# Attention with P turned by DVE in 32x32 blocks, and the context summed in sixteen 32x32 tiles

## The reference

```python
def _lora_linear(x, W, A, B):
    return x @ W + SCALING * (x @ A @ B)
q = _lora_linear(hidden_states, Wq, Aq, Bq).reshape(bsz, q_len, NH, HD)
...
k = _lora_linear(traces, Wk, Ak, Bk).reshape(bsz, t_len, NKV, HD)
v = _lora_linear(traces, Wv, Av, Bv).reshape(bsz, t_len, NKV, HD)
...
scores = jnp.einsum('bhqd,bhtd->bhqt', q, k) / jnp.sqrt(jnp.asarray(HD, q.dtype))
attn = jax.nn.softmax(scores, axis=-1)
context = jnp.einsum('bhqt,bhtd->bhqd', attn, v)
context = jnp.transpose(context, (0, 2, 1, 3)).reshape(bsz, q_len, H)
out = _lora_linear(context, Wo, Ao, Bo)
return hidden_states + out
```

## Time and profile before

| | us |
|---|---|
| median of 3 runs (755.91 to 757.85) | 755.97 |
| span of the profiled execution | 753.1 |
| PE busy | 737.6 |
| DVE busy | 469.0 |
| ACT busy | 382.0 |
| POOL busy | 349.1 |
| second pass of the body loop (127.98 to 193.53) | 65.55 |

### The profile page before, as it was taken

The page is one execution under the profiler, slowest core; times in us unless marked ns, Lnnn a source line. Parts: engine busy times, 40 slices in busy tenths (PEclk is TensorE's granted clock), DMA queues, the critical chain, the costliest instruction groups (busy, mean ns, idle before and its releaser), DMA issues.

```text
span 753.1 us, 17856 instructions
## 1 busy us (share of the span) xinstructions
PE 737.6 (98%) x5776; PEld 645.2 (86%) x5776; DVE 469.0 (62%) x988; ACT 382.0 (51%) x1287; POOL 349.1 (46%) x322
## 2 busy tenths in 40 slices
PE   7899999999999999999999999999999999999998
PEld 6678899889989989999998998999867788888886
DVE  5957687687768668767876866787696412212211
ACT  4437665666666666666666666665685210111100
POOL 4757645745654574565557457555766100000000
PEclk9999999999999999999999999999999999999999
DMA  7775544554453555345454544645464834343331
GB/s 257 271 219 164 169 140 140 159 172 122 139 174 126 157 152 163 119 139 175 138 156 149 155 131 128 172 139 178 139 181 154 276 130 156 117 167 111 111 111 56
DMA packets 94665, 117.01 MB, mean 155 GB/s; under 512 B 8624, under 2 KB 76208, under 8 KB 94640
## 3 DMA queue, kind: packets, MB, share of 16 engines
q1 hardware_dynamic: 94640, 116.69, 49.3%
HBM read 78.91 MB, written 37.75 MB: 155 GB/s over the span
## 4 chain that ended last, share of the span: by engine, by line
PE 88%; DVE 5%; DMA 2%; issue 2%; POOL 1%; ACT 0%; SPq 0%; POOLq 0%; DVEq 0%
PE banks L868 32%; PE banks L917 23%; PE banks L897 15%; PE banks L906 8%; PE banks L882 7%; DVE neg_max L718 2%; PE banks L853 2%; DVE x_lo L725 2%; DMA probs_t<-wq 1%; PE banks L855 1%; DMA probs<-b4q 1%; DMA probs_t<-b4kv 1%; POOL k_stack L510 1%; DVE lora L679 0%; DVE probs_t L263 0%
## 5 line engine op out<-in xcount | busy, mean ns | idle before, releaser
L525 POOL TENSOR_TENSOR probs<-probs,rsums 128x512 f32<-128x512 f32 x256 | 266.4, 1041 | 205.4 <-DVE rsums L750 204.6
L582 ACT ACTIVATE probs<-banks,neg_max 128x256 f32<-128x256 f32 x512 | 238.7, 475 | 175.7 <-DVE neg_max L718 170.8
L718 DVE TENSOR_REDUCE neg_max<-banks 128x2 f32<-128x512 f32 x256 | 174.3, 682 | 20.0 <-PE banks L882 20.0
L897 PE MATMUL banks<-ident,probs 128*128 128x128 f32 x1024 | 157.1, 276 | 2.2 <-POOL probs L525 2.0
L263 DVE COPY probs_t<-banks 128x512 f32<-128x512 f32 x192 | 132.4, 690 | 43.0 <-PE banks L897 35.6
L868 PE MATMUL banks<-x_hi,w_hi 128*128 128x256 f32 x512 | 145.7, 285 | 0.8 <-POOL w_lo L500 0.4
L868 PE MATMUL banks<-x_hi,w_lo 128*128 128x256 f32 x512 | 144.6, 282 | 0.0
L868 PE MATMUL banks<-x_lo,w_hi 128*128 128x256 f32 x512 | 144.5, 282 | 0.0
L897 PEld LDWEIGHTS banks<-ident,probs 128*128 128x128 f32 x1024 | 115.5, 140 | 30.8 <-issue 27.1
L882 PE MATMUL banks<-k_stack,q_stack 96*128 96x256 f32 x512 | 122.8, 322 | 0.0
L582 ACT ACTIVATION_READ_ACCUMULATOR probs<-banks,neg_max 128x1 f32 x512 | 104.0, 203 | 0.0
(11 more groups left out here) (76 smaller groups left out, 1112.9 us busy)
## 6 DMA issues: line engine op xcount, KB each, us to landing
q_stack<-q_parts SPq DMA_DIRECT2D x192, 128.0 KB, 2.5
q_parts<-q_stage SPq DMA_DIRECT2D x64, 256.0 KB, 2.2
raw<-ct SPq DMA_DIRECT2D x32, 256.0 KB, 3.9
raw<-xt SPq DMA_DIRECT2D x32, 256.0 KB, 4.4
context<-ctx_stage SPq DMA_DIRECT2D x64, 128.0 KB, 1.8
probs<-xn SPq DMA_DIRECT2D x16, 512.0 KB, 4.1
out<-raw SPq DMA_DIRECT2D x15, 512.0 KB, 2.9
probs_t<-context SPq DMA_DIRECT2D x7, 1024.0 KB, 5.9
```

The lines of the kernel that those rows point to most:

```text
L525: nc.gpsimd.tensor_tensor(probs[:, c], probs[:, c], rsums[:, c, :].unsqueeze(2).broadcast_to([P, 2, S]), ALU.mult).then_inc(norm_done, 1)
L582: last = nc.scalar.activation(probs[:, c, h, :], score_bank[c][:, S * h:S * (h + 1)], ACT.Exp, bias=neg_max[:, c, h:h + 1], scale=-1.0, ac ...
L718: nc.vector.tensor_reduce(out=neg_max[:, c, :], in_=score_bank[c].rearrange("p (h t) -> p h t", h=2), axis=AXIS, op=ALU.min).then_inc(max_ ...
L897: last = nc.tensor.transpose(bank[:, P * (2 * t + h):P * (2 * t + h + 1)], probs[:, c, h, P * t:P * (t + 1)], ident[:])
```

## The change

P is no longer turned by PE. DVE turns each 32x32 block of a slot's tile in place of its row and column (`transpose`, from `probs` to `turned_p`), so that partition 32r + t holds query block r, and each block of 32 keys has its 32 keys on 32 partitions. The four row groups of the array then belong to four blocks of 32 queries, the column groups to blocks of keys. `context_parts` makes, for a unit, 32 f32 matmuls of 32x32 by 256 columns: two turns of sixteen tiles. Row group r writes to bank r of four `part_bank`s; column group j sums key blocks j and 4 + j. ACT copies the four banks together (128x1024) to `parts`, and `context` adds the four column groups with `pick`, four identities of 32x32 under one another, in four 128x32 tiles. ACT copies that to `ctx_stage`. For the row groups V must lie four times under itself (`v_rep`): DVE writes it to `v_stage`, SP stores it to `v_rows` and loads it with eight transfers a batch.

Four banks of PSUM go to the partial sums, so scores have two, with `AHEAD = 2` and `NORM_AHEAD = 1`. Scores of slot s+2 wait for the exps of slot s. The groups of a batch stand in another order (v earlier, and q 3 in its place at the seam), and SP's transfers with them. Output steps no longer stand between slots; they follow the last slot, around the last `context_parts` and `context`.

```diff
-AHEAD = 4
-NORM_AHEAD = 3
+AHEAD = 2
+NORM_AHEAD = 1
...
 BODY = [("q", 4, 0), ("q", 5, 0), ("k", 0, 1), ("q", 6, 0), ("q", 7, 0), ("k", 1, 1),
-        ("q", 0, 1), ("q", 1, 1), ("q", 2, 1), ("q", 3, 1), ("v", 0, 1), ("v", 1, 1)]
+        ("q", 0, 1), ("q", 1, 1), ("v", 0, 1), ("v", 1, 1), ("q", 2, 1), ("q", 3, 1)]
...
-        score_bank = [banks[:, i, :] for i in range(4)]
-        turn_bank = [banks[:, 4 + i, :] for i in range(2)]
+        score_bank = [banks[:, i, :] for i in range(2)]
+        part_bank = [banks[:, 2 + i, 0:S] for i in range(4)]
+        ctx_bank = banks[:, 2, S:2 * S]
...
+            def load_v(m, fills, contexts):
+                cols = slice(P * m, P * (m + 1))
+                wait(v_stored, fills * DMA)
+                if contexts is not None:
+                    wait(parts_mm, parts_count(contexts))
+                for r in range(4):
+                    sp.dma_start(v_rep[32 * r:32 * (r + 1), :, cols],
+                                 v_dram[:, cols].rearrange("(k p) n -> p k n", p=32)).then_inc(v_in[m], DMA)
...
+                send_v(group0 + (pos["v", 1, 1] + 1))
+                load_v(0, b + 2, unit0 + 4)
+                store_ctx(7)
                 send(pos["q", 2, 1])
-                store_ctx(6)
-                send(pos["q", 3, 1])
+                load_v(1, b + 2, unit0 + 8)
                 stack_q(2, fills + 6, score0 + 36)
-                store_ctx(7)
...
                 if not (last and s + AHEAD >= SLOTS):
-                    act.wait_ge(turned, n + (s + 1))
-                    exps(n + (s + AHEAD), c)
+                    if s + AHEAD >= 4:
+                        act.wait_ge(turned, n + (s + AHEAD - 3))
+                    exps(n + (s + AHEAD), (s + AHEAD) % 4)
+                if c == 1 and not prologue:
+                    act.wait_ge(parts_mm, b * NG + parts_count(unit))
+                    nc.scalar.activation(parts[:], banks[:, 2:6, 0:S], ACT.Copy).then_inc(parts_done, 1)
...
+                if not (last and s >= SLOTS):
+                    dve.wait_ge(norm_done, n + (s + 1))
+                    if c == 0 and not prologue:
+                        dve.wait_ge(parts_mm, b * NG + parts_count(unit - 1))
+                    nc.vector.transpose(turned_p[:, unit % 2, c].rearrange("p h k q -> p (h k q)"),
+                                        probs[:, c].rearrange("p h t -> p (h t)")).then_inc(turned, 1)
...
+                for turn in range(KB // 4):
+                    for j in range(4):
+                        for r in range(4):
+                            rows = slice(32 * r, 32 * (r + 1))
+                            last = nc.tensor.matmul(
+                                part_bank[r][HD * j:HD * (j + 1), :],
+                                v_rep[rows, 4 * turn + j, HD * u:HD * (u + 1)],
+                                turned_p[rows, u % 2].rearrange("p c h k q -> p k (c h) q")[:, 4 * turn + j],
+                                start=(turn == 0), stop=(turn == KB // 4 - 1), tile_position=(32 * r, HD * j))
+                last.then_inc(parts_mm, 1)
+
+            def context(b, u):
+
+                pe.wait_ge(parts_done, b * NG + (u + 1))
+                pe.sem_inc(pe_waits, 1)
+                for h in range(GH):
+                    moving = parts[:].rearrange("p r (a h q) -> p h a r q", a=2, h=GH)
+                    last = nc.tensor.matmul(ctx_bank[HD * h:HD * (h + 1), :], pick[:], moving[:, h],
+                                            start=True, stop=True, tile_position=(0, HD * h))
...
+            for k in range(GROUP_MM):
+                out_step(0, 0, 0, k)
+            context_parts(NB - 1, NG - 1)
+            for k in range(GROUP_MM):
+                out_step(0, 1, 0, k)
+            context(NB - 1, NG - 1)
```

238 lines of the change are left out of this document (115 added, 123 removed).

## The result

The changed kernel takes 876.24 us (872.11 to 879.17, 4 runs) against 756.17 beside it: 1.158 times the time of before, interval 1.155 to 1.162. The forecast of 739 was wrong by 137 us, and on the wrong side of the kernel before. The profiled execution has a span of 872.4 us.

A forecast was written before the change was run, and what follows sets the result against it. TensorE, busy 98% of the span, was taken as the bound. From a span of 753.1 us, seven passes save 18.6 and the last pass adds 1.5: 736.0, with 2.9 around it about 739; range 728 to 790.

The forecast's parts named there:

- (4): ACT's eviction of the parts stands behind exps, so the selection matmul waits 0.5 us; a unit is 7.6, a pass 61.0.
- (6): Shorter queues of scores and normalisation: c_lo beside normalisation costs 1.3 us a pass, x_lo subtractions on DVE 0.6; pass 62.9.
- (1): PE loses 16 transposes a unit: a slot becomes 1.32 us, four slots 5.28.
- (2): Partial sums on PE, 64 records of 32x32: 1.17 us a unit if all sixteen tiles work at once.
- (3): Selection matmuls on PE, 8 records on four tiles in two rounds: 0.65 us a unit.
- The price of 25 ns a start: Skill page's floor on matmul starts: partial sums 1.6 us, 0.65 a unit more, kernel about 780; chance 0.05 within a rival.
- Rival B: Array doesn't run sixteen tiles at once: eight give 790 us, four 900; slower once partial sums exceed 1.45; chance 0.17.
- (5): DVE swaps three copies and an eviction a unit for four transposes of 128x512, taken at 0.7 us each; no bound.
- Rival D: Scores two ahead are too few: each unit loses 0.3 us more, 758, the same or a little slower; chance 0.14.
- (7): V's trip through memory, one store and eight loads a pass on SP's queue: priced at nothing, cover 2.5 us.
- (8): Last pass: fills gain 1.3 us, folds paced by DVE cost 0.8, output after the last fold 2; together +1.5.
- C: DVE's transpose runs at half rate, 1.22 us, making DVE the bound: 768, slower; chance 0.20.

The follow-up runs named there:

- the last kernel: Projection groups reordered to v0, q0, q1, v1, q2, q3 and each SP transfer placed where its data are ready, against the 755.25 us kernel: 743.40 us.
- the kernel with three edits: Changed kernel with PE's loop written out, ct loads issued a pass ahead and the parts eviction put ahead of the two exps: 821.24 us, ratio 1.085.
- V once: Changed kernel with V stored and loaded once ahead of the loop, so later batches use the first batch's V: 851.51 us.

## Why the prediction was wrong, step by step

**The work was priced right, its order was not.** A pass was forecast at 62.9. The changed kernel takes 80.1; with the same work in another order, PE's loop written out and two subtractions on another engine, it takes 61.5 to 62.9 and the whole 743. The 17.2 us a pass that were missed are, from the trace: 12.0 at the seam, 4.4 in the plain units (eight times 8.17, less the 61.0 of step (4)) and 1.6 in the unit with x_lo, less the 1.3 for c_lo; 0.5 is spread over other units. That 743 lies near 739 does not bear the forecast out: it is another kernel, and its passes lack the waits of (4), (6) and the seam by other means. Up to the end of the first pass 14.4 us are missed, in the six others 103 and in the last 20; the output gives 1 back.

**(1), (2), (3)** The mechanism was right, the sizes off. In the unit shown, the block is 1.42 instead of 1.17, four slots are 1.41 to 1.42 each instead of 1.32, the selection 0.57 instead of 0.65: 0.55 together. The block's first 32 records start as step (2) has it, sixteen within 0.10 us and sixteen more 0.24 behind them. Of the second 32 nearly all start one by one, some 17 ns apart, and there the 0.25 are lost; why is not known. The price of 25 ns a start, 1.6 for the block, is not met either. Rival B's break-even of 1.45 was missed by 0.03 only. With the 0.52 of (4) the plain unit is 8.17, that of before 8.15: the gain of 0.27 a unit that rival B counts on was gone before the seams.

**(4)** Right in size: the wait was forecast at 0.5 and is 0.52 (288.61 to 290.54 is 1.93, a slot 1.41). To put the eviction ahead gave the 0.52 back.

**(5)** Right, 693 ns; the high price of 1.24 is not met. **Rival D**, the short lead, was named with 0.3 a unit; in plain units it costs nothing, but it is why each delay of an input, a stack or a subtraction reached PE at once.

**(6)** For c_lo too dear, for x_lo too cheap. c_lo's slots lie at the seam of the changed kernel, where its price can't be told apart; in the last kernel the unit that has them takes 7.68 to 7.71 where nothing disturbs it, against 7.65. For x_lo 0.6 a pass was forecast, and its unit takes 2.2 more. The 830 ns of the earlier trace rows are a mean of two prices. Of the kernel before (shortest, median, longest):

```profile
L725 DVE TENSOR_TENSOR x_lo<-raw,x_hi x32: 675/681/2109, 27.7 to 494.8; 128x512 fp32r<-128x512 f32 x32
```

In each pass three took 0.68, and the one that began while POOL multiplied took 1.16 (295.48, POOL from 295.05 to 296.09). In the changed kernel all four of a pass begin beside POOL and take 1.13. A slot of DVE is then 2.3 to 2.7 (starts at 260.98, 263.66, 266.00, 268.67), not 2.05, two of them with a q_stage or k_stage of 0.41 besides. And PE's fills wait for x_lo themselves (11.8 us), which the step did not ask.

**(7)** This is the step that failed most. "I price it at nothing; its cover is 2.5 us." It looked at V's landing only. That was waited for 12 us in all (in the kernel with three edits). V's transfers, 2.8 and 3.0 us of issues at a seam, also held up what stood behind them: q's stack and the ct loads, which ACT waits for with exps and evictions in its order. What it priced at nothing is, in runs: 25 us with V once, 29 with the ct loads moved, and 26 more with the queue reordered in the kernel with three edits. The question "who waits for what is queued behind" was put for engines, not for SP's queue.

**The missing term.** No step asked how long PE's program is. A unit has 40 matmul records more (64 + 8 - 16 - 16) and as many weight loads, and the loop went from 1320 to 1939 instructions. Its branches back take 24.9 us in the changed kernel; 12 of them come back with the loop written out, since SP's queue covers the rest, and a branch costs up to 4.4 in the kernel before with two passes a turn. The prediction's last sentence named a lower granted clock as a sign that all would be wrong; it was 0.91 to 0.94 in the looped passes, and it fell behind standstills of PE, those at the branch and those for ACT alike (0.50 and 0.59 in the two windows).

**(8)** +1.5 forecast, 21.8 measured. The last pass begins with the same seam: its two units were 8.9 and 15.9, and the four loads of the first context were worth 6.4 us where they were moved. How the rest divides between the folds and the last unit, 17.2 us, was not tested.

**Chances.** 0.40 was given to slower, but with other mechanisms: that it turned slower bears none of B, C and D out. 876 lies outside 728 to 790, and none of the rivals was about a seam.

## What to carry to other kernels

Price a change by what it puts into a queue, not only by what it puts on an engine: for every transfer added, read who waits for the ones behind it, and for every wait in a queue, whether what stands behind it is ready earlier. When a change shortens the leads between stages, every fixed order in the kernel has to be laid out anew: here that, a loop written out and two subtractions moved made 133 us, with no operation less. A change that measures as a loss may be one that has not been scheduled yet. Count the instructions of a loop body: one that is no longer kept pays at each branch back, and then runs at half the clock for a while.

## What the runs showed of the hardware

- A PE loop of 1320 or 1427 instructions branches back in 0.2 us; in one of 1939 the branch takes 3.5 to 5.2 us and the matmuls stand still 3.8 on the mean of six (23.0 in all), in one of 2640 it takes 3.7 to 3.9. The instruction queue's packets rise from 14 or 15 to 75 and 48. Behind the pause the granted clock was 0.50 over 5 us.
- Sixteen tiles of 32x32 do work at once: their records start within 0.10 us and the next sixteen 0.24 later, as the rounds of four tiles of the earlier trace rows. But the second 32 records are dearer than the first: the block takes 0.64 us with 32 and 1.42 with 64.
- The DVE transpose of 128x512 f32 in blocks of 32x32 takes 693 ns, as the copy of the earlier trace rows.
- A DVE subtraction of two 128x512 f32 tiles in SBUF takes 0.68 us with POOL idle and 1.13 to 1.16 where it begins while POOL multiplies.
- Loads put early into an idle queue are not free: at a DMA share of 0.95 the first stack landed late and the first partial sums began 6 us later.
